# One PSUM tensor in an eight-layer attention kernel: key, value and attention rows made by one VectorE instruction over two banks instead of two

## The reference, cut to what matters

```
q = phi(h @ wq + bq);  k = phi(h @ wk + bk);  v = h @ wv + bv        # phi = elu + 1
kv = einsum('bshd,bshm->bhdm', k, v)
z = 1.0 / (einsum('bshd,bhd->bsh', q, k.sum(axis=1)) + 1e-06)
att = einsum('bshd,bhdm,bsh->bshm', q, kv, z)
h = ln(h + att @ wo + bo, g1, be1)
h = ln(h + gelu(h @ w1 + c1) @ w2 + c2, g2, be2)
```

## Time and profile before

| what | value |
|---|---|
| runs, median (lowest to highest) | 1097.68 us (1095.01 to 1098.82) |
| profiled execution, span from first to last instruction | 1097.7 us |
| mean granted TensorE clock | 0.970 |
| PE busy | 1017.6 us, 93% of the span |
| DVE busy | 790.8 us, 72% |
| ACT busy | 834.7 us, 76% |
| POOL busy | 767.4 us, 70% |

### The profile page before, as it was taken

The page is one execution under the profiler, slowest core; times in us unless marked ns, Lnnn a source line. Parts: engine busy times, 40 slices in busy tenths (PEclk is TensorE's granted clock), DMA queues, the critical chain, the costliest instruction groups (busy, mean ns, idle before and its releaser), DMA issues.

```text
span 1097.7 us, 25115 instructions
## 1 busy us (share of the span) xinstructions
PE 1017.6 (93%) x7766; PEld 957.2 (87%) x7766; DVE 790.8 (72%) x2850; ACT 834.7 (76%) x1621; POOL 767.4 (70%) x1157
## 2 busy tenths in 40 slices
PE   5799899999999999999999999999999859889983
PEld 4798899999999999999999999999988749889983
DVE  6777677777777777777777777777788988933514
ACT  6777788888788888888888888888886746555572
POOL 5958877677767767776777677776675676757742
PEclk9999999999999999999999999999998969979997
DMA  4100010080008003500530075200000346557684
GB/s 136 50 1 16 20 50 2 15 164 15 1 19 165 11 1 68 115 12 15 96 83 1 16 129 139 40 1 2 1 1 1 99 144 185 148 164 217 203 256 149
DMA packets 85154, 81.00 MB, mean 74 GB/s; under 512 B 6780, under 2 KB 66179, under 8 KB 85024
## 3 DMA queue, kind: packets, MB, share of 16 engines
q1 hardware_dynamic: 80480, 70.93, 26.1%
q0 software_dynamic: 4544, 8.47, 2.2%
HBM read 44.82 MB, written 29.44 MB: 68 GB/s over the span
## 4 chain that ended last, share of the span: by engine, by line
PE 70%; DVE 9%; POOL 8%; issue 5%; ACT 3%; SPq 3%; DMA 2%; POOLq 0%; DVEq 0%
PE ps L1828 17%; PE ps L1705 8%; PE ps L1707 8%; PE ps L1706 8%; PE ps L1758 7%; PE ps L1752 5%; PE ps L1786 5%; PE ps L1985 4%; PE ps L1969 4%; PE ps L1740 2%; ACT s L948 1%; DVE x_lo L1233 1%; POOL xs L856 1%; POOL rstd L685 1%; DVE stat L1151 1%
## 5 line engine op out<-in xcount | busy, mean ns | idle before, releaser
L948 ACT ACTIVATE s<-s,shift,rstd 128x128 f32<-128x128 f32 x496 | 203.9, 485 | 50.1 <-POOL shift L687 48.9
L1828 PE MATMUL ps<-this_w,hid 128*128 128x128 f32 x1792 | 214.3, 275 | 0.0
L1828 PEld LDWEIGHTS ps<-this_w,hid 128*128 128x128 f32 x1792 | 206.9, 192 | 0.0
L932 ACT ACTIVATE hid<-ps,col 128x512 f32<-128x512 f32 x256 | 155.2, 684 | 2.4 <-PE ps L1707 2.1
L685 POOL TENSOR_TENSOR rstd<-var,neg_half 128x4 f32<-128x4 f32 x132 | 144.5, 1095 | 11.0
L728 POOL TENSOR_TENSOR res_a<-s,row 128x512 f32<-128x512 f32 x60 | 76.8, 1280 | 72.3 <-ACT s L948 67.5
L682 POOL TENSOR_SCALAR shift<-mv 128x4 f32<-128x4 f32 x132 | 26.9, 203 | 123.4 <-DVE mv L1155 123.3
L1151 DVE BATCH_NORM_STATS2 stat<-s 128x6 f32<-128x128 f32 x512 | 110.2, 276 | 0.0
L1705 PE MATMUL ps<-x_hi,this_w 128*128 128x512 f32 x224 | 95.3, 425 | 1.2 <-DVE x_lo L1233 1.2
L713 POOL TENSOR_TENSOR res_f<-res_f,row 128x512 f32<-128x512 f32 x64 | 92.1, 1438 | 5.0
L1985 PE MATMUL ps<-heads,hid 128*128 x624 | 87.3, 285 | 5.1 <-ACT hid L1077 4.5
(11 more groups left out here) (261 smaller groups left out, 2788.5 us busy)
## 6 DMA issues: line engine op xcount, KB each, us to landing
xs<-pad SPq DMA_DIRECT2D x6, 2925.0 KB, 18.0
res_a<-w SPq DMA_DIRECT2D x40, 256.0 KB
xblk<-xs SPq DMA_DIRECT2D x78, 65.0 KB
raw_w<-w SPq DMA_DIRECT2D x18, 256.0 KB, 7.3
row<-rows SPq DMA_DIRECT2D x8, 512.0 KB, 4.8
this_w<-next_w SPq DMA_DIRECT2D x7, 512.0 KB, 3.2
third_w<-w SPq DMA_DIRECT2D x10, 256.0 KB, 17.2
scaled_w<-w SPq DMA_DIRECT2D x10, 256.0 KB
```

The source lines that it names most:

```text
L932: a.activation(hid[h][:, c, :], ps(3 + h + c), ACT.Gelu, bias=col[:, bass.ds(lw * FF + (C_C1 + c), 1)]).then_inc(hid_done, 1)
L948: ins = a.activation(dst[:, t, :], src[:, t, :], ACT.Identity, bias=shift[i][:, t:t + 1], scale=rstd[i][:, t:t + 1])
L1828: ins = t_.matmul(ps(down_bank(l, s, h))[:, t * P:(t + 1) * P], hid[h][:, c, t * P:(t + 1) * P], down[:, c, :], start=c == 0, stop=c == FF ...
```

## The change

The four PSUM tensors become one of eight banks. A function `pair_tiles(b)` gives the two banks from b on as four tiles with one stride of 256 elements. With that, the key rows, the value rows and the attention rows of a half are each one DVE instruction over four tiles, where they were two over two tiles; that one carries the semaphore's increment. The attention matmuls write tile t at the start of its half bank; before, the second tile of a bank began at element 144.

```diff
-        bank = [ctx.enter_context(nc.psum_tensor("ps01", [P, 2, 512], F32)),
...
+        psum = ctx.enter_context(nc.psum_tensor("psum", [P, 8, 512], F32))

         def ps(b):
-            return bank[b // 2][:, b % 2, :]
+            return psum[:, b, :]
+
+        def pair_tiles(b):
+
+            return psum[:, b:b + 2, :].rearrange("p b (t n) -> p (b t) n", t=2)
@@ keys_values
-                for half in two:
-                    b = (1, 4)[h] + half
-                    src = ps(b).rearrange("p (t n) -> p t n", t=2)
-                    ins = d.tensor_tensor(kt[h][:, 2 * half:2 * half + 2, :], src[:, :, 0:P],
-                                          row[:, ring, R_BK:R_BK + 1, :].to_broadcast([P, 2, P]), ALU.add)
-                ins.then_inc(kt_done, 1)
...
+                src = pair_tiles((1, 4)[h])
+                d.tensor_tensor(kt[h][:, :, :], src[:, :, 0:P],
+                                row[:, ring, R_BK:R_BK + 1, :].to_broadcast([P, T, P]), ALU.add).then_inc(kt_done, 1)
+                d.tensor_tensor(v[h][:, :, 0:P], src[:, :, P:2 * P],
+                                row[:, ring, R_BK + 1:R_BK + 2, :].to_broadcast([P, T, P]), ALU.add).then_inc(v_done, 1)
@@ attend
-                src = bank[h][:, :, 0:2 * KVW].rearrange("p b (t n) -> p b t n", t=2)
...
-                for b in two:
-                    ins = d.tensor_tensor(
-                        att[h][:, 2 * b:2 * b + 2, :].rearrange("p t (a c) -> p t a c", c=HEAD),
-                        src[:, b, :, 0:P].rearrange("p t (a c) -> p t a c", c=HEAD),
-                        rec[h][:, 2 * b:2 * b + 2, :].unsqueeze(3).to_broadcast([P, 2, HEADS, HEAD]), ALU.mult)
-                ins.then_inc(att_done, 1)
+                src = pair_tiles(2 * h)
...
+                d.tensor_tensor(att[h][:, :, :].rearrange("p t (a c) -> p t a c", c=HEAD),
+                                src[:, :, 0:P].rearrange("p t (a c) -> p t a c", c=HEAD),
+                                rec[h][:, :, :].unsqueeze(3).to_broadcast([P, T, HEADS, HEAD]), ALU.mult
+                                ).then_inc(att_done, 1)
@@ attention (PE)
-                    ins = t_.matmul(bank[h][:, t // 2, (t % 2) * KVW:(t % 2 + 1) * KVW], qt[h][:, t * P:(t + 1) * P],
+                    ins = t_.matmul(pair_tiles(2 * h)[:, t, 0:KVW], qt[h][:, t * P:(t + 1) * P],
                                     kv[h][:, t // 2, :], start=True, stop=True)
```

More of the change, by code:

```diff
@@ L172, in sem @@
             return ctx.enter_context(nc.semaphore(name))
-        bank = [ctx.enter_context(nc.psum_tensor("ps01", [P, 2, 512], F32)),
-                ctx.enter_context(nc.psum_tensor("ps23", [P, 2, 512], F32)),
-                ctx.enter_context(nc.psum_tensor("ps45", [P, 2, 512], F32)),
-                ctx.enter_context(nc.psum_tensor("ps67", [P, 2, 512], F32))]
+        psum = ctx.enter_context(nc.psum_tensor("psum", [P, 8, 512], F32))
         def ps(b):
-            return bank[b // 2][:, b % 2, :]
+            return psum[:, b, :]
+        def pair_tiles(b):
+            return psum[:, b:b + 2, :].rearrange("p b (t n) -> p (b t) n", t=2)
         x_all = sb("x_all", [P, HALVES, T, P])
@@ L1202, in attend @@
                 wait(dve, attt_mm, upto(l, s - 1, h))
-                src = bank[h][:, :, 0:2 * KVW].rearrange("p b (t n) -> p b t n", t=2)
-                d.tensor_scalar(den[h][:, :, :].rearrange("p (b t) c -> p b t c", b=2), src[:, :, :, P:KVW], DEN_EPS, None,
-                                ALU.add).then_inc(den_done, 1)
+                src = pair_tiles(2 * h)
+                d.tensor_scalar(den[h][:, :, :], src[:, :, P:KVW], DEN_EPS, None, ALU.add).then_inc(den_done, 1)
                 wait(dve, den_done, upto(l, s, h))
```

## The result

| | median of runs (lowest to highest) |
|---|---|
| before, in the same comparison | 1095.72 us (1094.38 to 1098.82), 6 runs |
| changed kernel | 1090.16 us (1088.21 to 1092.69), 6 runs |
| ratio | 0.9947, 95% interval 0.9929 to 0.9965 |

The change makes the kernel 0.53% faster, 5.6 us by the medians.

What follows compares the result with a forecast made beforehand. PE bounds the kernel, stopping once a slot for DVE's x_lo. Terms 3.25 (slots) + 0.26 (attention rows) + 0.10 (first slot) = 3.6 us off 1097.7 gave 1094.1 us, 0.33% faster; range 1091.3 to 1097.0.

Steps and rivals of the forecast that it cites:

- The loop: Each slot: PE's projection, key rows, value rows, statistics, POOL's row of work, keys(1), x_lo, PE's attention; half 0's merges count.
- through ACT: Rival: keys(1) is set by ACT's exp, so only earlier key rows count; 2.0 us off, 1095.7; chance 0.17.
- The price of a merge: DVE, one instruction for two: 0.065 us a merge, 0.13 us for half 0's key and value rows per slot.
- The 125 ns: Rival: a merge saves the Trainium skill's fixed PSUM-to-SBUF cost on DVE; 6.9 us off, 1090.8; chance 0.05.
- The lock: DVE instructions with two SBUF inputs and POOL's exclude each other; keys(1) ends 0.55 us behind POOL's multiply L711.
- The slots: Half 0's key and value rows save 0.13 us in each of 25 slots with the stop: 3.25 us.
- the stop: PE's wait for DVE's x_lo before the attention matmuls (L1752), 0.17 to 0.33 us a slot, all a slot can give.
- The terms of 0.26 us (attention rows) and 0.10 (first slot): Attention rows save 2 x 0.13 us in the fourth and last slots; the first slot's key pairs save 0.10 us.
- The base: The 3.6 us were taken off a profiled span of 1097.7 us, called the median of the runs (1097.68).
- the rivals' gains: ACT alone 1095.7 (0.17), larger price about 1090.8 (0.05), no gain 1097.5 (0.14), slower in either way (0.06).
- What was said to show it: 64 instructions of about 0.69 us per kind, L1752's wait down to about 2, keys(1) still 0.55 behind L711.
- The cover: Half 1's merges save 0.13 us before keys(1), where DVE waits for ACT's exp anyway; that wait grows, worth nothing.

Runs made afterwards that it cites:

- first pair: First profiles of the kernel before and the changed kernel; from the fifth slot to the last the changed kernel is 3.8 us ahead.
- second pair: Second profiles of the kernel before and the changed kernel, both word for word; from the fifth slot to the last the changed kernel is 3.9 us ahead.
- second comparison: The changed kernel and the kernel before, both word for word, run again: ratio 0.9962 (0.9948 to 0.9976), which is 4.2 us.

## Why the prediction was right and wrong

**The loop: right.** In an undisturbed slot two of the six merges count, those of half 0, and the others are covered. Half 0 alone gives 3.6 of 3.7 us (some 0.5 of it in the eighth and ninth slots, where any merge does), half 1 and the attention rows nothing in an undisturbed slot. That the way leads through POOL's row and its hold on keys(1), not through ACT, is shown by the value rows alone and by the split multiply.

**The price of a merge: right.** 0.13 us for the pair of merges was taken, 0.13 is what the timelines show. The 125 ns of the errata section of "VectorE: DVE Perf Modes" (the Trainium skill), which would have made 0.25, is not what back-to-back instructions pay here: start to start two of 256 elements took 0.67 us and one of 512 takes 0.61 (406.86 - 406.25), 0.06 between them.

**The lock: right.** The rule of "SBUF — State Buffer", "Who interferes with whom" (the Trainium skill), that the one that started first keeps the other out for its whole instruction, agrees with the trace: from the second to the 31st slot keys(1) ends 0.54 to 0.60 us behind the end of the POOL instruction that was running when it started, in all ten profiles, and the split turned the order. Where the two start within 20 ns of each other it does not hold to the letter (last section).

**The slots: 3.25 us taken, 3.7 us measured, with one stop left out.** "25 x 0.13 = 3.25" counted the rows of the wait view. That view leaves out short gaps: in the changed kernel it names x_lo 3 times for 0.8 us, though nearly every middle slot still has the stop, now on the weight loads as 7.4 us in 27 times:

```profile
PEld psum L1743 <- issue: 7.4, 27, 0.5
```

Per slot the 0.13 us held, and nearly every slot of the stretch has it. The second and third slots, ahead of the stretch, are 0.13 to 0.14 us shorter too, in both pairs of profiles. What the sum did not have is PE's wait for ACT's normalization in the eighth slot, worth 0.5 us. Together that is 3.9 us in the first pair and 4.1 in the second, where I had 3.6. The terms of 0.26 us (attention rows) and 0.10 (first slot) cannot be told from chance: in the ten profiles the fourth slot takes 28.7 to 31.4 us, the last one 32.0 to 32.9, and the first attention starts between 26.6 and 28.6. For the same reason the 4.37 us of the first pair is no measure of the change; the second pair has 5.73 at the same place. The second comparison's 4.2 us and the first one's 5.6 both have 3.9 to 4.1 in their intervals.

**The base: wrong, and the step that took the result out of the range.** "The sum is ... off a profiled span of 1097.7, which is the median of the runs (1097.68)." Both halves of the sentence failed. A run is about 1.7 us longer than its span (the changed kernel's profiled run took 1088.21 with a span of 1086.5), so a span of 1097.7 would be a run of some 1099.4, above all three that were given, and the half clock behind 965 us is in it. And the median of three runs, 1097.68, was high: the same three with three more gave 1095.72, and other runs of that kernel 1095.37 (34 runs), 1094.67 (23) and 1094.01 (10). From 1095.72 the same 3.6 us would have been 1092.1 with 1089.3 to 1095.0 as the range, and the measured 1090.16 lies in it. From 1097.68 even a gain of 4.1 us would have left it out, by 0.7 us. Of the 3.9 us between forecast and result about half are the base, 2.0; the other half are the gain, 5.6 by the medians for 3.6, of which the slots show 0.3 to 0.5 and the second comparison 0.6. The range had been made from the rivals' gains alone; the base was taken as exact, although the three runs lay 3.8 us apart.

**What was said to show it.** Sizes, spacing and the 0.55 us came as said. The wait of L1752 for x_lo fell to 0.8 us and not to about 2, since the gaps that are left are too short for that view; PE's idle time in front of L1752, 5.3 us before and 3.1 after, tells more. The wait for exp in front of keys(1) did not grow: 0.52 us for 0.53. The time saved on half 1 went into another wait, one step earlier: `mask_kv(0)` (L1188) now waits 0.20 us for PE, 10.2 us idle in the run and 8.0 of it for PE (3.9 and 2.6 before). The cover was right, the place was not.

## What to carry to other kernels

Merging small VectorE instructions was worth 0.06 us each here, and in an undisturbed slot only where the pair lies on the loop that ends the stop of the bound engine: follow that loop back over the engines before counting merges. Where an instruction's duration differs between slots, compare its end with the ends on the engine that may be holding it; cutting the other engine's long instruction in two gave as much again here (3.6 us in the stretch) as all the merges (3.7). And take the base of a forecast from many runs, with its own width in the range, when single executions lie as far apart as the gain.

## What the runs showed of the hardware that I had not expected

Which of DVE and POOL goes first can hang on a few nanoseconds. In the last slot keys(1) and POOL's add L713 start together in four of the ten profiles. Before, DVE and POOL:

```profile
836.86 1.82 DVE L1186 SCALAR_TENSOR_TENSOR kt<-kt,heads 128x512 f32<-128x512 f32 x1
...
836.85 1.28 POOL L713 TENSOR_TENSOR res_f<-res_f,row 128x512 f32<-128x512 f32 x1
```

After:

```profile
832.76 0.68 DVE L1180 SCALAR_TENSOR_TENSOR kt<-kt,heads 128x512 f32<-128x512 f32 x1
...
832.75 1.84 POOL L714 TENSOR_TENSOR res_f<-res_f,row 128x512 f32<-128x512 f32 x1
```

POOL's start was 16 ns earlier in the one and 14 ns in the other, and the order was the opposite: 1.82 us for DVE there, 0.68 here. The other two profiles fit: with the value rows alone POOL started 20 ns earlier and went first, and with half 0 alone it started 7 ns earlier and DVE went first, though it was the later one.

```profile
837.20 1.81 DVE L1186 SCALAR_TENSOR_TENSOR kt<-kt,heads 128x512 f32<-128x512 f32 x1
833.58 0.68 DVE L1187 SCALAR_TENSOR_TENSOR kt<-kt,heads 128x512 f32<-128x512 f32 x1
```
